# Storing the item product with the tiles innermost, so that the weights of a matmul lie 312 bytes apart

## The chip, the cores and the metric

The kernel runs on one core of one Trainium2 chip. The metric is the device time in microseconds (us), here always of that single core. TensorE does the matmuls and loads their weights (in the profile PE and PEld), VectorE is DVE, ScalarE is ACT, GpSimd is POOL, and SyncE (SP) issues most of the transfers from HBM.

## The reference

One layer of a graph network over 10000 users and 10000 items, with 128 features, all in float32:

```python
h = jnp.maximum(_layernorm(x, axis=-1), 0.0)          # [10000 users, 128]
# in the layer: user_feat = h, adj is [10000, 10000]
h = item_feat @ W_item.T + b_item                     # the item product
b = user_feat @ W_user.T + b_user
return jax.nn.relu(adj @ h + b)
# and outside: x = x + that
```

The adjacency matrix has 400 MB, and `adj @ h` is nearly all of the work.

## The kernel before

The result is made transposed: features on the 128 partitions, users along the free dimension. The users are cut into 5 groups of 2000 columns, and a group into four banks of 500 columns (`acc[0]` to `acc[3]` in PSUM). The items are cut into 78 tiles of 128, called chunks in the code, and 16 left over. For a group, TensorE goes through the 78 chunks and adds each chunk's part to all four banks.

To keep float32 precision with the `fp32r` type of TensorE, both factors are split into a high and a low part. SyncE loads an adjacency tile of 128x2000 into `a_ring` (six slots). ScalarE casts it into `hi_ring` (L277), VectorE writes the difference into `lo_ring` (L340); both rings have three slots. TensorE then does twelve matmuls of 500 columns a chunk, four for each of three products: `h_lo` by `hi_ring`, `h_hi` by `hi_ring` (both L508), `h_hi` by `lo_ring` (L514). The weights, which TensorE loads before each matmul, are `h_lo[:, c, :]` or `h_hi[:, c, :]`: for chunk `c`, 128 items on the partitions and 128 features along the free dimension. When the last of the twelve is done, the slot comes free for ScalarE.

`h_hi` and `h_lo` are the two parts of the item product. They are made once, during the first group, three chunks (a trio) at a time: three float32 matmuls L464 into a PSUM bank (each shows as two matmul rows with two weight loads), L345 on VectorE adds the bias into `h_full`, L282 on ScalarE casts it into `h_hi`, and L352 on VectorE writes `h_full - h_hi` into `h_lo`. TensorE makes the product of a trio two trios before it uses it. The other four groups only read `h_hi` and `h_lo`.

Beside that runs the layer norm of `x`, in four units a group, one in each 12 chunks. Its TensorE part is four transposes of `x` (L484), four of the normed rows (L490) and a float32 matmul with `W_user` (L497). Where the trio's matmuls L464 and the one with `W_user` fall on one chunk, L464 comes first. A group ends with the matmuls of the 16 items left over (L525), and VectorE adds the relu of the banks to `x` in `y` (L397); the first four matmuls of the next group wait for that, bank by bank.

The order on each engine is that in which the code is written; no planner chooses it. The changed lines are the two allocations of `h_hi` and `h_lo` (L104, L105). What writes them is L282 and L352, what reads them L352, L508 and L514.

Of the kernel before, what the change touches and what calls it, by code (L numbers as in the profile page):

```python
# [29 lines left out]
P = 128  # L30
N_USER = 10000
N_ITEM = 10000
HID = 128
# [10 lines left out]
CHUNKS = N_ITEM // P  # L44
# [28 lines left out]
F32R = mybir.dt.float32r  # L73
# [19 lines left out]
def graph_layer(nc, adj_tiles, adj_rem, ones_row, item_t, x_rows, w_item_t, b_item_rows, w_user_t, b_user, out_t):  # L93
    with ExitStack() as ctx:  # L94
        def sb(name, shape, dt=F32):
            return ctx.enter_context(nc.sbuf_tensor(name, shape, dt))
# [4 lines left out]
        a_ring = sb("a_ring", [P, A_SLOTS, PITCH])  # L101
        hi_ring = sb("hi_ring", [P, S_SLOTS, GROUP_W], F32R)
        lo_ring = sb("lo_ring", [P, S_SLOTS, GROUP_W], F32R)
        h_hi = sb("h_hi", [P, CHUNKS, HID], F32R)  # L104
        h_lo = sb("h_lo", [P, CHUNKS, HID], F32R)  # L105

        a_rem = sb("a_rem", [P, BANK_W])
        h_rem = sb("h_rem", [P, HID])
# [459 lines left out]
```

## Time and profile before

| | |
|---|---|
| three runs | 1153.7, 1154.68, 1154.87 us; median 1154.68 |
| the profiled execution | 1155.03 us, of which the span from first to last instruction is 1153.5 |
| mean granted TensorE clock | 0.997 |
| PE busy | 1132.1 us, 98% of the span, 5078 matmuls |
| PEld busy | 925.8 us, 80%, 5078 weight loads |
| DVE busy | 976.4 us, 85% |
| ACT busy | 773.4 us, 67% |
| read from HBM | 410.45 MB, 360 GB/s over the span |

The profile comes from one execution. A matmul's row is longer than what a matmul takes in a stream of them, because the rows of matmuls that follow each other overlap; so the step from one matmul to the next (the pitch) is read from how long a stretch of several lasts. Weight loads have rows of their own and lie beside the matmul before them. Where the trace's timeline merges rows that follow each other, "x4" is their count, and the time is from the start of the first to the end of the last.

### The profile page before, as it was taken

How to read it: one execution, taken by the hardware profiler on the slowest of the kernel's cores; microseconds unless marked ns; L12 is line 12 of the kernel's file. 1: busy time of each engine (PE TensorE's matmuls, PEld its weight loads, DVE VectorE, ACT ScalarE, POOL GpSimd, SP SyncE). 2: the span in 40 equal slices, each digit the busy share in tenths (PEclk: the TensorE clock that was granted, in tenths of full speed). 3: DMA queues.
4: the chain of work that ended last, by engine and by line, in shares of the span. 5: the costliest groups of instructions: out<-in, count | busy, mean ns of one | idle time of the engine just before them, and what ended most of it. 6: DMA issues, size and time to landing. Idle time of an engine off the chain costs nothing.

```text
span 1153.5 us, 14338 instructions
## 1 busy us (share of the span) xinstructions
PE 1132.1 (98%) x5078; PEld 925.8 (80%) x5078; DVE 976.4 (85%) x683; ACT 773.4 (67%) x502; POOL 20.3 (2%) x42
## 2 busy tenths in 40 slices
PE   6999999999999999999999999999999999999998
PEld 5888888878888888788888887888888878888886
DVE  5989988888888888898898888888888888888886
ACT  4766767667676666576667675766666657667663
POOL 0000000000000000000000000000000000000000
PEclk9999999999999999999999999999999999999999
DMA  9999999999999999999999998999999999999993
GB/s 355 397 400 359 352 364 372 347 362 345 376 372 360 367 365 392 365 370 368 355 367 362 385 379 338 376 362 373 357 371 380 381 331 378 376 358 353 364 387 120
DMA packets 62659, 416.38 MB, mean 361 GB/s; under 512 B 7644, under 2 KB 9124, under 8 KB 62608
## 3 DMA queue, kind: packets, MB, share of 16 engines
q1 hardware_dynamic: 59984, 406.38, 92.3%
q0 software_dynamic: 2624, 9.22, 2.3%
q8 instruction: 44, 0.72, 0.2%
q14 instruction: 7, 0.06, 0.0%
HBM read 410.45 MB, written 5.12 MB: 360 GB/s over the span
## 4 chain that ended last, share of the span: by engine, by line
PE 96%; DVE 1%; issue 1%; ACT 1%; DMA 1%; DVEq 0%; SPq 0%; ACTq 0%
PE acc L508 61%; PE acc L514 31%; PE spare L464 2%; PE acc L497 1%; DVE y L397 1%; PE spare L490 1%; PE spare L484 1%; ACT hi_ring L277 1%; DMA items<-in_item_t 1%; DVE lo_ring L340 0%; PE acc L525 0%; DVEq L94 0%; DVEq L427 0%; SPq L199 0%; SPq L188 0%
## 5 line engine op out<-in xcount | busy, mean ns | idle before, releaser
L340 DVE TENSOR_TENSOR lo_ring<-a_ring,hi_ring 128x2000 fp32r<-128x2000 f32 x390 | 871.3, 2241 | 152.8 <-ACT hi_ring L277 151.4
L277 ACT CAST hi_ring<-a_ring 128x2000 fp32r<-128x2000 f32 x390 | 729.0, 1869 | 360.6 <-PE acc L514 357.2
L508 PE MATMUL acc<-hi_ring,h_lo 128*128 128x500 f32 x1560 | 434.6, 399 | 5.5 <-DVE y L397 4.4
L508 PE MATMUL acc<-hi_ring,h_hi 128*128 128x500 f32 x1560 | 420.0, 391 | 0.0
L514 PE MATMUL acc<-lo_ring,h_hi 128*128 128x500 f32 x1560 | 419.1, 390 | 0.0
L508 PEld LDWEIGHTS acc<-hi_ring,h_lo 128*128 128x128 f32 x1560 | 289.5, 189 | 76.4 <-DVE y L397 12.4
L514 PEld LDWEIGHTS acc<-lo_ring,h_hi 128*128 128x128 f32 x1560 | 294.2, 189 | 62.1
L508 PEld LDWEIGHTS acc<-hi_ring,h_hi 128*128 128x128 f32 x1560 | 293.9, 188 | 61.7
L464 PE MATMUL spare<-wi,items 128*128 128x128 f32 x156 | 23.9, 294 | 10.5 <-DMA items<-in_item_t 8.7
L464 PEld LDWEIGHTS spare<-wi,items 128*128 128x128 f32 x156 | 23.0, 206 | 12.9 <-issue 6.8
L345 DVE TENSOR_TENSOR h_full<-spare,bi 128x384 f32<-128x384 f32 x26 | 14.3, 551 | 10.3 <-DMA bi<-in_b_item_rows 6.6
L245 POOL DMA_DIRECT2D rows<-in_x_rows x20 | 10.9, 544 | 595.3 <-PE spare L484 595.0
L497 PE MATMUL acc<-normed_t,wu 128*128 128x500 f32 x40 | 20.0, 581 | 0.0
L282 ACT CAST h_hi<-h_full 128x384 fp32r<-128x384 f32 x26 | 13.2, 507 | 5.5 <-DVE h_full L345 5.5
L397 DVE SCALAR_TENSOR_TENSOR y<-acc,y 128x500 f32<-128x500 f32 x20 | 12.1, 670 | 5.1 <-PE acc L525 5.1
L258 POOL DMA_DIRECT2D out_t<-y x16 | 8.8, 548 | 400.5 <-DVE y L397 399.8
L352 DVE TENSOR_TENSOR h_lo<-h_full,h_hi 128x384 fp32r<-128x384 f32 x26 | 14.4, 552 | 0.6 <-ACT h_hi L282 0.6
L364 DVE TENSOR_TENSOR centred<-rows,stat 125x512 f32<-125x512 f32 x20 | 13.9, 693 | 0.7
L387 DVE SCALAR_TENSOR_TENSOR normed<-centred,stat 125x512 f32<-125x512 f32 x20 | 13.8, 692 | 0.7
L370 DVE TENSOR_REDUCE stat<-squares 125x4 f32<-125x512 f32 x20 | 13.6, 679 | 0.0
L360 DVE TENSOR_REDUCE stat<-rows 125x4 f32<-125x512 f32 x20 | 13.6, 678 | 0.0
L287 ACT ACTIVATE squares<-centred 125x512 f32<-125x512 f32 x20 | 12.5, 627 | 0.0
(29 smaller groups left out, 113.8 us busy)
## 6 DMA issues: line engine op xcount, KB each, us to landing
a_ring<-in_adj_tiles SPq DMA_DIRECT2D x390, 1000.0 KB, 6.9
rows<-in_x_rows POOLq DMA_DIRECT2D x20, 250.0 KB, 7.6
items<-in_item_t SPq DMA_DIRECT2D x12, 384.0 KB, 7.6
out_t<-y POOLq DMA_DIRECT2D x16, 250.0 KB, 5.3
out_t<-y SPq DMA_DIRECT2D x4, 250.0 KB, 2.2
a_rem<-in_adj_rem SPq DMA_DIRECT2D x20, 31.2 KB, 4.2
items<-in_item_t SPq DMA_DIRECT2D x2, 192.0 KB, 4.9
wi<-in_w_item_t SPq DMA_DIRECT2D x1, 64.0 KB, 1.8
```

The lines of the kernel that those rows point to most:

```text
L277: nc.scalar.copy(hi_ring[:, r, :], a_ring[:, s, 0:GROUP_W]).then_inc(hi_written, 1)
L340: nc.vector.tensor_tensor(lo_ring[:, r, :], a_ring[:, s, 0:GROUP_W], hi_ring[:, r, :], ALU.subtract).then_inc(lo_written[s], 1)
L345: nc.vector.tensor_tensor(h_full[:, trio % H_BANKS, :, :], h_banks[trio % H_BANKS][:, 0:TRIO_W].rearrange("p (c d) -> p c d", d=HID), bi[: ...
L352: nc.vector.tensor_tensor(h_lo[:, trio * TRIO:(trio + 1) * TRIO, :], h_full[:, trio % H_BANKS, :, :], h_hi[:, trio * TRIO:(trio + 1) * TRI ...
L360: nc.vector.reduce_sum(total, rows[:, :, :], AX_X).then_inc(chain, 1)
L364: nc.vector.tensor_tensor(centred[:, :, :], rows[:, :, :], mean.unsqueeze(2).broadcast_to(wide), ALU.subtract).then_inc(centred_ready, 1)
L387: nc.vector.scalar_tensor_tensor(out=normed[:, :, :], in0=centred[:, :, :], scalar=0.0, in1=rstd.unsqueeze(2).broadcast_to(wide), op0=ALU.max,
L397: nc.vector.scalar_tensor_tensor(out=cols, in0=acc[k][:, 0:BANK_W], scalar=0.0, in1=cols, op0=ALU.max, op1=ALU.add).then_inc(y_ready[k], 1)
L464: last = nc.tensor.matmul(bank[:, m * HID:(m + 1) * HID], items[:, slot, at:at + P], wi[:, :], start=(m == 0), stop=True, skip_group_check ...
L497: nc.tensor.matmul(acc[k][:, 0:BANK_W], wu[:, :], normed_t[:, :], start=False, stop=False, skip_group_check=True)
L508: nc.tensor.matmul(acc[k][:, 0:BANK_W], h_part[:, c, :], hi_ring[:, r, k * BANK_W:(k + 1) * BANK_W], start=(c == 0 and h_part is h_lo), st ...
L514: last = nc.tensor.matmul(acc[k][:, 0:BANK_W], h_hi[:, c, :], lo_ring[:, r, k * BANK_W:(k + 1) * BANK_W], start=False, stop=False, skip_gr ...
```

## The change

The two tiles have their dimensions in another order: before, `[128 partitions, 78 chunks, 128 features]`, so that the 128 features of a chunk lie side by side, 4 bytes apart. Now they are `[128 partitions, 128 features, 78 chunks]`, so that the 78 chunks of one feature lie side by side, and the features of one chunk 78 x 4 = 312 bytes apart. The names `h_hi` and `h_lo` are now rearranged views with the old order of indices, so that every line that uses them stays as it is. The size in memory is the same, 39,936 bytes a partition for each of the two.

```diff
-        h_hi = sb("h_hi", [P, CHUNKS, HID], F32R)
-        h_lo = sb("h_lo", [P, CHUNKS, HID], F32R)
+        h_hi_cols = sb("h_hi_cols", [P, HID, CHUNKS], F32R)
+        h_lo_cols = sb("h_lo_cols", [P, HID, CHUNKS], F32R)
+        h_hi, h_lo = h_hi_cols[:, :, :].rearrange("p d c -> p c d"), h_lo_cols[:, :, :].rearrange("p d c -> p c d")
```

No instruction is added, removed or moved on any engine. In the profile of the changed kernel the tiles are called `h_hi_cols` and `h_lo_cols`, and each line after L105 has a number one higher.

## Rows read from the trace of the kernel before

**Rows 1.** The page: busy time, and the chain that ended last.
```profile
PE 1132.1 (98%) x5078; PEld 925.8 (80%) x5078; DVE 976.4 (85%) x683; ACT 773.4 (67%) x502; POOL 20.3 (2%) x42
PE 96%; DVE 1%; issue 1%; ACT 1%; DMA 1%; DVEq 0%; SPq 0%; ACTq 0%
```

**Rows 2.** The page's groups: line, engine, operation, shapes, count | busy us, mean ns | idle before.
```profile
L340 DVE TENSOR_TENSOR lo_ring<-a_ring,hi_ring 128x2000 fp32r<-128x2000 f32 x390 | 871.3, 2241 | 152.8 <-ACT hi_ring L277 151.4
L277 ACT CAST hi_ring<-a_ring 128x2000 fp32r<-128x2000 f32 x390 | 729.0, 1869 | 360.6 <-PE acc L514 357.2
...
L508 PEld LDWEIGHTS acc<-hi_ring,h_lo 128*128 128x128 f32 x1560 | 289.5, 189 | 76.4 <-DVE y L397 12.4
L514 PEld LDWEIGHTS acc<-lo_ring,h_hi 128*128 128x128 f32 x1560 | 294.2, 189 | 62.1
L508 PEld LDWEIGHTS acc<-hi_ring,h_hi 128*128 128x128 f32 x1560 | 293.9, 188 | 61.7
```

**Rows 3.** Timeline of PE in the third group: start us, us, line, count.
```profile
602.39 1.06 PE L508 MATMUL acc<-hi_ring,h_hi 128*128 128x500 f32 x4
603.29 1.07 PE L514 MATMUL acc<-lo_ring,h_hi 128*128 128x500 f32 x4
604.21 1.07 PE L508 MATMUL acc<-hi_ring,h_lo 128*128 128x500 f32 x4
605.12 1.06 PE L508 MATMUL acc<-hi_ring,h_hi 128*128 128x500 f32 x4
606.02 1.07 PE L514 MATMUL acc<-lo_ring,h_hi 128*128 128x500 f32 x4
```

**Rows 4.** Longest L508 matmul (min/median/max ns); timeline near the start, before the clock rose.
```profile
L508 PE MATMUL acc<-hi_ring,h_hi x1560: 384/389/620, 16.8 to 1145.7; 128*128 128x500 f32 x195
...
16.82 1.87 PE L508 MATMUL acc<-hi_ring,h_hi 128*128 128x500 f32 x4
...
16.41 1.58 PEld L508 LDWEIGHTS acc<-hi_ring,h_hi 128*128 128x128 f32 x4
```

**Rows 5.** Weight loads by line (L508, L477, L484): ns min/median/max; 128, 16, 128 columns.
```profile
L508 PEld LDWEIGHTS acc<-hi_ring,h_lo x1560: 186/188/334, 14.9 to 1144.6; 128*128 128x128 f32 x195
...
L477 PEld LDWEIGHTS spare<-wi,items_rem x2: 93/94/96, 243.8 to 243.8; 128*16 128x16 f32 x2
...
L484 PEld LDWEIGHTS spare<-ident,rows x4: 137/139/142, 600.8 to 601.3; 125*128 125x128 f32 x4
```

**Rows 6.** One trio's item product and what follows it: durations of L464, timeline of PE and PEld.
```profile
L464 PE MATMUL spare<-wi,items x6: 270/275/275, 25.3 to 25.9; 128*128 128x128 f32 x6
...
25.30 0.83 PE L464 MATMUL spare<-wi,items 128*128 128x128 f32 x6
25.88 1.16 PE L508 MATMUL acc<-hi_ring,h_lo 128*128 128x500 f32 x4
26.88 1.07 PE L508 MATMUL acc<-hi_ring,h_hi 128*128 128x500 f32 x4
...
25.08 0.86 PEld L464 LDWEIGHTS spare<-wi,items 128*128 128x128 f32 x6
25.85 0.76 PEld L508 LDWEIGHTS acc<-hi_ring,h_lo 128*128 128x128 f32 x4
```

**Rows 7.** Matmuls of the transposes and of `W_user`: durations, timeline of PE.
```profile
L484 PE MATMUL spare<-ident,rows x4: 267/268/270, 601.1 to 601.4; 125*128 125x125 f32 x4
...
601.07 0.59 PE L484 MATMUL spare<-ident,rows 125*128 125x125 f32 x4
601.41 1.14 PE L508 MATMUL acc<-hi_ring,h_lo 128*128 128x500 f32 x4
...
71.08 1.00 PE L497 MATMUL acc<-normed_t,wu 128*128 128x500 f32 x2
...
L497 PE MATMUL acc<-normed_t,wu 128*128 128x500 f32 x40 | 20.0, 581 | 0.0
```

**Rows 8.** Start of the second group, the last of the four waits of L508.
```profile
256.50 0.19 PEld L508 LDWEIGHTS acc<-hi_ring,h_lo 128*128 128x128 f32 x1 [0.40 <-DVE y L397]
```

**Rows 9.** Groups that touch the tiles once, and the slowest row an element.
```profile
L352 DVE TENSOR_TENSOR h_lo<-h_full,h_hi 128x384 fp32r<-128x384 f32 x26 | 14.4, 552 | 0.6 <-ACT h_hi L282 0.6
...
L282 ACT CAST h_hi<-h_full 128x384 fp32r<-128x384 f32 x26 | 13.2, 507 | 5.5 <-DVE h_full L345 5.5
...
L241 POOL TENSOR_SCALAR_AFFINE_SELECT ident<-ident 125x125 f32<-125x125 f32 x1 | 0.3, 287 | 0.2 <-POOL ident L239 0.2
```

**Rows 10.** Windows, one layer-norm unit of the first group: stretch, PE, PEld, DVE, ACT, POOL busy us.
```profile
50.00:86.70 36.70, 36.70 (x178) 30.58 (x177) 33.52 (x32) 25.45 (x20) 0.53 (x1) 1.00 1.01 403
```

## The prediction

> **What bounds the kernel now.** I read the chain of waits first. It lies on TensorE for 96% of the span, and TensorE is busy for 98% of it [rows 1]. The groups say the same from the other side: ScalarE sat idle for 357 us until TensorE gave a slot back, and VectorE for 151 us until ScalarE had cast [rows 2]. So both have slack, and the adjacency tiles, which wait for VectorE, come in time. The time is the number of matmuls by their pitch.
>
> The pitch comes from the timeline. From 603.29 to 606.02, one whole chunk, are 12 matmuls in 2.73 us, so 0.2275 us each [rows 3]. 4680 matmuls (3 x 1560) by that are 1065 us of the 1153.5; the rest is the first 15 us, the item product, the layer norm and the turns of the groups.
>
> Each matmul has a weight load of 189 ns [rows 2], which lies under the matmul before it. This load is what the change touches, 4680 times, and the question is how much longer it may become before it shows. Its row splits in two. 128 columns take 188 ns and 16 columns 94 ns [rows 5], so a column takes (188 - 94) / 112 = 0.84 ns, 128 of them 107 ns, and 81 ns are fixed. The fixed part does not add to the pitch: in the item product, L464, six matmuls and their six loads of 128 columns go at (0.83 - 0.275) / 5 = 0.111 us each [rows 6], though each load's row is as long as any other. So loads can follow each other at the time of their columns plus at most 4 ns. In the main stream a load may thus grow from 107 to about 223 ns of columns (2.1 times) before the pitch of 227 moves.
>
> **The price of a column 312 bytes from the next.** No row of the trace has such a read by TensorE, so I bound it. The low end is no change, 0.84 ns. For it speaks that the loads of the transposes, also 128 columns of float32, take 139 ns [rows 5], by the same fixed part 0.45 ns a column: what brings the weights can go twice as fast as L508 and L514 ask, and has something to lose before a load is longer. For the high end I take the slowest rate an element of any row, GpSimd's select, 287 / 125 = 2.3 ns with its start counted in [rows 9]. The middle of the two is 1.57 ns. I take a doubling, 1.68 ns, which is the nearest whole step: a load's columns then take 213 ns and its row 189 + 107, about 295 ns.
>
> Two pages of the Trainium skill bear on this, and they pull apart. "SBUF — State Buffer" (the note on cachelines) has lines of 16 bytes and wants at least two hits in each for full speed; at 312 bytes every column is in a line of its own. "Vector Engine (DVE) Microarchitecture Reference" (The SBUF access granule) gives VectorE prices for hops at every element, 1.73 to 1.76 ns at most distances and 2.50 at one of 96 bytes; if TensorE paid the first, a load would have 224 ns of columns and the pitch would just move, and at 2.50 it would be 325 ns. "TensorE: Matmul & The Clock Gate" (LDWEIGHTS) on the other hand gives the load as its columns over 1.2 GHz, with nothing about distance; by it the sum is zero. The trace agrees with that page on 107 ns, but only for words that lie side by side.
>
> **The change part by part, at the doubled column.**
>
> Main stream: 213 + 4 = 217 ns of load against a pitch of 227. It stays hidden, with 10 ns to spare: 0. At the low end 0 too. At the high end 128 x 2.3 + 4 = 298 ns is 71 ns over the pitch, and 4680 x 71 ns = 332 us.
>
> After short matmuls: here the cover is thin. The first load of L508 after the item product starts at 25.85, with the last matmul of L464, which lasts 107 to 111 ns; the next load already starts 0.11 us later, since four loads take 0.76 us here and 0.87 elsewhere [rows 6]. A load of 213 ns has about 106 ns uncovered, and TensorE pays them, since it is the bound. The same holds behind the transposes: (0.59 - 0.27) / 3 = 0.107 us each, and the first L508 stands directly behind [rows 7]. The places: 24 trios in the first group's loop, less the four (chunks 18, 30, 42 and 54) where the matmul of `W_user` comes between, are 20; 1 for the 16 items left over (L477); 20 behind L484 and 20 behind L490. 61 places by 0.107 us are 6.5 us. The four where L497 comes between cost nothing, since that matmul has a pitch of (1.00 - 0.58) = 0.42 us [rows 7]. At the low end this is 0, at the high end 61 x (298 - 111) ns = 11 us.
>
> Group turns: the load of the first L508 of each bank waits for VectorE and starts only then [rows 8]. The first three lie beside VectorE's next bank (0.40 us of idle time between); the last delays the chain by 0.107 us. 4 turns: 0.4 us.
>
> Before the clock rose: at the granted half clock (1.2 of 2.4 GHz) four matmuls take 1.87 us, a pitch of (1.87 - 0.62) / 3 = 0.417, with loads whose row is 333 ns [rows 4]. A load has 0.417 us of cover there. 0.
>
> The writers: L282 on ScalarE and L352 on VectorE now write, and L352 also reads, with 312 bytes between elements, 384 elements, 26 times each. VectorE's rate is 2241 / 2000 = 1.12 ns and ScalarE's 0.93 [rows 2]. At the low end nothing; at 2.3 ns, 0.45 us more for L352 and 0.53 for L282. In a layer-norm unit of the first group, 36.7 us with four trios, VectorE is busy for 33.5 and ScalarE for 25.5 [rows 10]. VectorE has 3.2 us to spare against 4 x 0.45 = 1.8, ScalarE 11.2 against 2.1. Their results are also wanted two trios later, 17 us. Hidden: 0. Were VectorE's cover gone in the four units, it would be up to 4 x 1.8 = 7 us. The first trio's casts are done before the first adjacency tile has come.
>
> The sum: 0 + 6.5 + 0.4 = 6.9 us on the profiled execution's 1155.03, gives 1161.9. The median of the runs is 0.35 us below the profiled one, so 1161.6.
>
> **The rivals.**
>
> *The columns cost what they cost now.* The reserve of two in the path of the weights [rows 5] covers the distance. Loads stay at 189 ns, and the time is 1154.7, give or take 1. For it speaks the 0.45 ns of the transposes; against it that these read neighbouring words too. 0.31.
>
> *The load becomes the bound of the main stream.* From 1.74 ns a column on (223 / 128), the pitch is the load's. This is a second mechanism beside my small term, and it has a steep price: each tenth of a nanosecond a column is 12.8 ns a matmul, 60 us. At three times the present column, 320 + 4 = 324 ns, it is 97 ns by 4680, 454 us, and with the places behind short matmuls (61 x 213 ns = 13 us) 1622. For it speaks that the doubled value lies only 3% under the point where it begins. Just above it, at 1.78 ns, it would be 23 us more, 1185. 0.12 for just above (1165 to 1200), 0.10 for far above.
>
> *The load disturbs the matmul's own reading.* 500 columns at 2.4 GHz are 208 ns, and the pitch is 227; at half clock it is 417, 500 columns at 1.2 GHz [rows 3, 4]. So something takes 19 ns a matmul at the full clock. If that is the load taking turns with the moving columns, a load that takes twice as long would take twice the turns: 19 x 4680 = 89 us more, 1251 with the 6.9; a third of that gives 1191. Against it: the matmuls with float32 columns show just 4 or 5 ns over their columns with as many loads, though at half the rate. 0.09.
>
> *Faster.* The same 19 ns may be a conflict between neighbouring words, which another layout may relieve; a tenth of it, 2 ns a matmul, is 9 us less, 1146. Nothing in the profile points to it. 0.04.
>
> *The change doesn't do what it says.* The rows of each engine are the same in kind and number, and a hidden copy into the old layout would have to be an instruction. Within the 0.31.
>
> **How the numbers follow.** My forecast, doubled or partly raised columns with the exposed places, has 0.34: 1158 to 1164 (at 1.3 ns a column the exposed part is half, some 3.5 us). Columns as now 0.31, just above the pitch 0.12, far above 0.10, disturbance 0.09, faster 0.04. A measurement of this kernel tells 0.2%, 2.3 us, from no change. Slower than that: 0.34 + 0.12 + 0.10 + 0.09 = 0.65; within: 0.31; faster: 0.04. The range reaches from 1152 to 1230: it holds the two likeliest, the load just above the pitch and a third of the disturbance, together 0.80. The likeliest one's own range is 1158 to 1164.
>
> **What would show it.** The loads of L509 and L515 (one line lower in the new file) at about 295 ns and those of L464 still at 192; the main stream still at 2.73 us a chunk; the four loads of the first L509 behind L464 no longer shorter than the others; L352 and L282 longer, without a wait behind them. If the load's row stays at 189, the first rival is right and all of my term goes. If a chunk takes more than 2.75 us, one of the two expensive rivals holds: the load as bound if its row is over 305 ns, disturbance if it is not.

## The result: slower by 7%, and the profile after

| | before | changed |
|---|---|---|
| timed runs, median | 1154.78 us (1153.7 to 1155.36) | 1236.02 us (1235.25 to 1237.7) |
| profiled execution, and its span | 1155.03, 1153.5 us | 1235.25, 1233.7 us |
| PE busy | 1132.1 us, 98% | 1214.5 us, 98% |
| PEld busy | 925.8 us, 80% | 1193.4 us, 97% |
| DVE, ACT busy | 976.4, 773.4 us | 984.7, 785.3 us |

The ratio is 1.0708, with a 95% interval from 1.0692 to 1.0724. The forecast was 1161.6 us, with a range up to 1230.

The groups of the page after answer to [rows 2] and [rows 9] (line, engine, operation, shapes, count | busy us, mean ns | idle before):

```profile
L509 PEld LDWEIGHTS acc<-hi_ring,h_lo_cols 128*128 128x128 f32 x1560 | 415.9, 331 | 17.1 <-DVE y L398 10.1
L509 PEld LDWEIGHTS acc<-hi_ring,h_hi_cols 128*128 128x128 f32 x1560 | 415.4, 332 | 0.5
L515 PEld LDWEIGHTS acc<-lo_ring,h_hi_cols 128*128 128x128 f32 x1560 | 415.3, 332 | 0.3
L465 PEld LDWEIGHTS spare<-wi,items 128*128 128x128 f32 x156 | 23.3, 208 | 11.7 <-issue 7.4
...
L283 ACT CAST h_hi_cols<-h_full 128x384 fp32r<-128x384 f32 x26 | 23.3, 897 | 6.1 <-DVE h_full L346 6.1
L353 DVE TENSOR_TENSOR h_lo_cols<-h_full,h_hi_cols 128x384 fp32r<-128x384 f32 x26 | 22.7, 872 | 0.9 <-ACT h_hi_cols L283 0.9
```

A weight load of the changed tiles takes 332 ns instead of 189; the loads of L465, whose weights lie side by side, are as before. Before, the loads of L514 had 62 us of gaps, now those of L515 have 0.3: a load follows a load without a gap. That fits loads that everything waits for, but does not show it: in the run at 12 bytes below the gaps are 0.3 us too, and there the loads are too short to be the bound. What shows it are the runs with fewer columns.

The timeline of one chunk in the fourth group (start us, us, line, count), to be laid beside [rows 3]:

```profile
803.16 1.14 PE L509 MATMUL acc<-hi_ring,h_lo_cols 128*128 128x500 f32 x4
804.14 1.14 PE L509 MATMUL acc<-hi_ring,h_hi_cols 128*128 128x500 f32 x4
805.11 1.13 PE L515 MATMUL acc<-lo_ring,h_hi_cols 128*128 128x500 f32 x4
806.08 1.00 PE L498 MATMUL acc<-normed_t,wu 128*128 128x500 f32 x2
```

From 803.16 to 806.08 a chunk takes 2.92 us where it took 2.73, so the pitch is 243.3 ns instead of 227.5. 4680 x 15.8 ns are 74 us, give or take 4, since 0.01 us in a chunk is 4 us in all. Over the whole trace at full clock, the mean pitch of the matmuls in mid-stream went from 227.5 to 244.1 ns, which is 78 us. The places behind short matmuls (for [rows 6]):

```profile
25.23 1.33 PE L509 MATMUL acc<-hi_ring,h_lo_cols 128*128 128x500 f32 x4
26.40 1.14 PE L509 MATMUL acc<-hi_ring,h_hi_cols 128*128 128x500 f32 x4
```

Before, the four long matmuls behind L464 took 25.88 to 26.88, 1.00 us, where four others took 0.91; now they take 1.17, where four others take 0.97. That is 0.11 us lost beyond the main stream's share. Over the 60 such places of the trace at full clock, the step from the first long matmul to the second went from 312 to 441 ns; less the 16 of any matmul this is 113 ns, 6.9 us for 61 places. With 0.4 us for the turns of the groups the terms are 78 + 6.9 + 0.4 = 85.

Against them stands the clock. TensorE's granted clock (third number from the end; 0.50 is 1.2 of 2.4 GHz) is half in two stretches inside the work before, and in one after:

```profile
702.20:705.50 3.30, 3.27 (x8) 2.67 (x9) 2.13 (x1) 0.00 (x0) 1.20 (x3) 0.50 0.99 385
927.50:930.80 3.30, 3.30 (x9) 2.63 (x9) 1.14 (x1) 0.75 (x1) 0.33 (x1) 0.50 1.00 385
...
273.20:276.50 3.30, 3.30 (x8) 2.57 (x9) 2.42 (x2) 0.00 (x0) 1.50 (x3) 0.50 0.95 361
```

The slow start also lasted until 19.4 us before and 17.2 after. That is 5.7 us less at half the pace, worth 2.6 us (an estimate from the pitches of 417 and 227.5 ns). Some 82 us are thus expected and the spans differ by 80.2; the last 2 were not found. VectorE's wait for ScalarE grew from 151 to 224 us, ScalarE's for TensorE from 357 to 425, both by having more slack.

### The profile page after: what moved, and what is told of

It is laid out like the page before. It is cut to its first block, busy times and chain, and to the rows that moved or that the text cites. A ratio compares the mean times of both kernels' runs of the same rounds, so it can differ in the third digit from the quotient of the medians.

```text
span 1233.7 us, 14338 instructions
## 1 busy us (share of the span) xinstructions
PE 1214.5 (98%) x5078; PEld 1193.4 (97%) x5078; DVE 984.7 (80%) x683; ACT 785.3 (64%) x502; POOL 20.4 (2%) x42
## 4 chain that ended last, share of the span: by engine, by line
PE 97%; issue 1%; ACT 1%; DMA 1%; DVE 1%; SPq 0%; DVEq 0%; ACTq 0%
PE acc L509 62%; PE acc L515 31%; PE spare L465 2%; PE acc L498 1%; PE spare L485 1%; PE spare L491 1%; ACT hi_ring L278 1%; DMA items<-in_item_t 1%; DVE y L398 0%; DVE lo_ring L341 0%; PE acc L526 0%; DVEq L94 0%; SPq L200 0%; SPq L189 0%; SPq L199 0%
## 5 line engine op out<-in xcount | busy, mean ns | idle before, releaser
L509 PE MATMUL acc<-hi_ring,h_lo_cols 128*128 128x500 f32 x1560 | 469.3, 423 | 3.6 <-DVE y L398 3.6
L509 PE MATMUL acc<-hi_ring,h_hi_cols 128*128 128x500 f32 x1560 | 444.6, 408 | 0.0
L515 PE MATMUL acc<-lo_ring,h_hi_cols 128*128 128x500 f32 x1560 | 444.2, 407 | 0.0
L509 PEld LDWEIGHTS acc<-hi_ring,h_lo_cols 128*128 128x128 f32 x1560 | 415.9, 331 | 17.1 <-DVE y L398 10.1
L509 PEld LDWEIGHTS acc<-hi_ring,h_hi_cols 128*128 128x128 f32 x1560 | 415.4, 332 | 0.5
L515 PEld LDWEIGHTS acc<-lo_ring,h_hi_cols 128*128 128x128 f32 x1560 | 415.3, 332 | 0.3
L465 PEld LDWEIGHTS spare<-wi,items 128*128 128x128 f32 x156 | 23.3, 208 | 11.7 <-issue 7.4
L465 PE MATMUL spare<-wi,items 128*128 128x128 f32 x156 | 24.0, 294 | 10.3 <-DMA items<-in_item_t 8.5
L283 ACT CAST h_hi_cols<-h_full 128x384 fp32r<-128x384 f32 x26 | 23.3, 897 | 6.1 <-DVE h_full L346 6.1
L353 DVE TENSOR_TENSOR h_lo_cols<-h_full,h_hi_cols 128x384 fp32r<-128x384 f32 x26 | 22.7, 872 | 0.9 <-ACT h_hi_cols L283 0.9
```

The lines of the kernel that those rows point to most:

```text
L283: nc.scalar.copy(h_hi[:, trio * TRIO:(trio + 1) * TRIO, :], h_full[:, trio % H_BANKS, :, :]).then_inc(h_hi_set, 1)
L353: nc.vector.tensor_tensor(h_lo[:, trio * TRIO:(trio + 1) * TRIO, :], h_full[:, trio % H_BANKS, :, :], h_hi[:, trio * TRIO:(trio + 1) * TRI ...
L465: last = nc.tensor.matmul(bank[:, m * HID:(m + 1) * HID], items[:, slot, at:at + P], wi[:, :], start=(m == 0), stop=True, skip_group_check ...
L509: nc.tensor.matmul(acc[k][:, 0:BANK_W], h_part[:, c, :], hi_ring[:, r, k * BANK_W:(k + 1) * BANK_W], start=(c == 0 and h_part is h_lo), st ...
L515: last = nc.tensor.matmul(acc[k][:, 0:BANK_W], h_hi[:, c, :], lo_ring[:, r, k * BANK_W:(k + 1) * BANK_W], start=False, stop=False, skip_gr ...
```

## The experiments

Two theories to begin with. A: the load is the bound; it needs about 1.9 ns a column, and the matmul waits for it. B: the load is hidden, but its separate reads disturb the reading of the 500 moving columns.

### One part alone

```diff
+        h_hi_cols = sb("h_hi_cols", [P, HID, CHUNKS], F32R)
+        h_hi = h_hi_cols[:, :, :].rearrange("p d c -> p c d")
```

and h_lo as before; the second run has it the other way round. Both compute the whole result.

> Only h_hi is stored with the tiles innermost, h_lo as before. Theory A (the strided load takes about 1.9 ns a column whatever else goes on, 244 ns for 128, and a matmul cannot start before its load is done): 3120 of 4680 matmuls go from 227 to 243.5 ns, +51 us; nothing at the places behind short matmuls, since there the first load is one of h_lo. 1206 us. Theory B (the strided load is hidden, but disturbs the reading of the 500 moving columns): also +51 us for the main stream; the two are not told apart here, it is the size of the parts that is. If the term behind short matmuls (6.9 us) doesn't exist, e1 and e2 together give the whole 81 us with 2 to 1 between them (1209 and 1182).

> Only h_lo is stored with the tiles innermost. Theory A: 1560 x 16.2 ns = 25 us, and the 61 places behind short matmuls and 4 group turns by 0.107 us, 6.9 us: 1155 + 32 = 1187 us. Without the term behind short matmuls 1180 to 1182.

Measured: 1203.27 us, ratio 1.0414 (1.0396 to 1.0431), and 1185.29 us, 1.0259 (1.0242 to 1.0276). That is 47.8 and 29.8 us, 77.6 together. Per matmul it is 15.3 ns for the 3120 of h_hi, and (29.8 - 6.9) / 1560 = 14.7 for h_lo, but 19.1 if the term behind short matmuls is left in: the shares are 1.6 to 1 and not 2 to 1. The timelines of PE behind L465 show the term itself, with h_hi alone and then with h_lo alone:

```profile
26.69 1.16 PE L509 MATMUL acc<-hi_ring,h_lo 128*128 128x500 f32 x4
27.69 1.14 PE L509 MATMUL acc<-hi_ring,h_hi_cols 128*128 128x500 f32 x4
```
```profile
25.19 1.33 PE L509 MATMUL acc<-hi_ring,h_lo_cols 128*128 128x500 f32 x4
26.35 1.06 PE L509 MATMUL acc<-hi_ring,h_hi 128*128 128x500 f32 x4
```

1.00 us as before the change, and 1.16 as after it: the term belongs to h_lo's loads, as expected. The halves add up to 3.6 us less than the whole. Both traces have one cheap step in each chunk, where the loads go over from the near part to the far one: it is 231 to 232 ns in the median and not 244, 390 times, 4.7 us in each run. In the changed kernel, which has far loads only, no such step is left.

### Theory A or B

The third product (L515) in the changed kernel with 128 of the 500 moving columns, the rest of that product left out:

```diff
-nc.tensor.matmul(acc[k][:, 0:BANK_W], h_hi[:, c, :], lo_ring[:, r, k * BANK_W:(k + 1) * BANK_W],
+nc.tensor.matmul(acc[k][:, 0:128], h_hi[:, c, :], lo_ring[:, r, k * BANK_W:k * BANK_W + 128],
```

> The changed kernel, but each matmul of the third product (lo_ring) streams only the first 128 of the 500 columns of its bank; the rest of that product is left out. Theory A: these matmuls still have a pitch of about 243 ns, since the load sets it, and the time stays at 1236 us. Theory B: with 128 columns to stream there is little left to disturb; their pitch falls to some 215 or less (the doubled load plus 4 ns), and the time to 1190 or less.

The time was 1225.14 us (ratio 1.0604, 1.0583 to 1.0626), nearer to theory A's 1236 than to theory B's 1190. One chunk in its timeline, PE and PEld:

```profile
805.83 0.97 PE L515 MATMUL acc<-lo_ring,h_hi_cols 128*128 128x128 f32 x4
806.63 1.31 PE L509 MATMUL acc<-hi_ring,h_lo_cols 128*128 128x500 f32 x4
807.77 1.14 PE L509 MATMUL acc<-hi_ring,h_hi_cols 128*128 128x500 f32 x4
808.75 0.97 PE L515 MATMUL acc<-lo_ring,h_hi_cols 128*128 128x128 f32 x4
...
805.59 1.06 PEld L515 LDWEIGHTS acc<-lo_ring,h_hi_cols 128*128 128x128 f32 x4
806.55 1.07 PEld L509 LDWEIGHTS acc<-hi_ring,h_lo_cols 128*128 128x128 f32 x4
```

The loads of L515 are (1.06 - 0.34) / 3 = 0.24 us apart (243 ns in the median over the trace), with a quarter of the columns to stream, and a chunk still takes 2.92 us, from 805.83 to 808.75. The 11 us that were saved lie where the stream changes to the short matmuls or to the next group: the stretch from the first load of L515 before such a change to the second long matmul behind it is 116 to 172 ns shorter in the median, 84 times, 11 us in all. Theory A holds at 312 bytes: the matmul has no part in the pitch.

Fewer weight columns, in the same line, are the other side of it:

```diff
+nc.tensor.matmul(acc[k][0:64, 0:BANK_W], h_hi[:, c, 0:64], lo_ring[:, r, k * BANK_W:(k + 1) * BANK_W],
```

and the same with 112 of the 128.

> The changed kernel, but each matmul of the third product loads only 64 of the 128 weight columns (and makes 64 of the 128 features; the rest of that product is left out). Theory A: a load of 64 strided columns takes 122 ns, its row about 205, well under a matmul of 227, so the 1560 matmuls that have such a load beside them go back to 227 ns: 1236 - 25 = 1211 us. Theory B: half the strided reads, half the disturbance: a pitch of 235 and 1223 us.

> The changed kernel (312 bytes), but each matmul of the third product loads only 112 of its 128 weight columns (and makes 112 features; the rest of that product is left out). With the load as bound, at 1.87 ns a column, 112 columns are done in 209 + 4 = 213 ns, below the matmul's 227. If the pitch of 243.7 is the load's alone, it falls at once to the 229 to 232 that the hidden strided loads show (64 columns, and 320 bytes): 1236 - 1560 x 13 ns = 1216 us. If the pitch follows the number of strided reads in proportion instead: 227 + 16.5 x 112 / 128 = 241.5, and 1233 us.

Both leave out the features whose weights are not loaded. Measured: 1214.13 us (ratio 1.0509, 1.0488 to 1.053) and 1218.37 (1.055, 1.0511 to 1.0589). The timeline of PE with 112 columns, and its loads on the page of groups with 64 and with 112:

```profile
806.50 1.09 PE L515 MATMUL acc<-lo_ring,h_hi_cols 128*112 128x500 f32 x4
807.42 1.14 PE L509 MATMUL acc<-hi_ring,h_lo_cols 128*128 128x500 f32 x4
```
```profile
L515 PEld LDWEIGHTS acc<-lo_ring,h_hi_cols 128*64 128x64 f32 x1560 | 313.5, 201 | 37.0 <-issue 1.1
```
```profile
L515 PEld LDWEIGHTS acc<-lo_ring,h_hi_cols 128*112 128x112 f32 x1560 | 388.2, 291 | 1.2
```

From 128 to 112 strided columns the pitch falls at once, from 243 to 0.92 / 4 = 230 ns here and 232 in the mean of the trace, and 112 down to 64 bring only 4 us more in 1560 matmuls, 3 ns each (229 in the mean; the times alone, two executions each, do not tell the two apart). That is a threshold, as theory A has it: 1216 was expected for it, and 1233 for a price in proportion.

The rows confirm the price. 81 + 64 x 1.87 = 201 ns and 81 + 112 x 1.87 = 290 are the rows of 201 and 291; 128 columns would have 320, and the row is 332. Where the loads are the bound, a row is thus some 12 ns longer than its fixed part and its columns.

### How far apart is far

All these compute the whole result; only the order in memory differs, so that the weights lie at other distances. Of each edit, the line that sets the order (the lines that use the tiles are adapted to it):

```diff
+ h_both = sb("h_both", [P, CHUNKS, HID, 2], F32R)          # 8 bytes, h_hi = [..., 0], h_lo = [..., 1]
+ h_hi = sb("h_hi", [P, TRIOS, HID, TRIO], F32R)            # 12 bytes, h_lo alike
+ h_both = sb("h_both", [P, TRIOS, HID, TRIO * 2], F32R)    # 24 bytes
+ h_hi = sb("h_hi", [P, HID, CHUNKS + 2], F32R)             # 320 bytes, h_lo alike
```

> h_hi and h_lo are stored interleaved, so that the 128 weights of a matmul lie 8 bytes apart: each line of 16 bytes still holds two of them. Theory L (lines: a load is slow when fewer than two of its columns share 16 bytes): loads stay at 189 ns, pitch 227, 1155 us. Theory N (neighbours: any column that is not adjacent to the one before costs about 1.9 ns): loads of 332 ns, pitch 243.5 and 1236 us.

> Three chunks are stored innermost, the weights of a matmul lie 12 bytes apart: 128 columns touch 96 lines of 16 bytes. Theory L: between the two; at 1.9 ns a line 96 lines are 182 ns, so the load's row grows to about 260 ns, which the matmul still hides; only the 61 places behind short matmuls show, 75 ns each: 1155 + 5 = 1160 us. Theory N: 1236 us.

> Three chunks and the two parts are stored innermost, the weights of a matmul lie 24 bytes apart, each in a line of its own. Theory L and theory N: as in the changed kernel, loads of 332 ns and 1236 us. If the distance itself matters (a price that grows with it), something between 1160 and 1230.

> As the changed kernel, but the row of chunks is padded from 78 to 80, so that the weights lie 320 bytes apart, a multiple of 16 and of 64, and all columns of a load lie at the same place in their line. If the price of 1.9 ns holds for any far column: 1236 us. If 312 bytes suffered from its odd alignment, less; if 320 meets a conflict between banks of the memory, far more (2.5 ns a column would be a pitch of 324 ns and 1620 us).

The first three went as the lines of 16 bytes would have it in their order, but not in size: 1160.33, 1167.41 and 1185.17 us, where theory L had 1155, 1160 and 1236. 320 bytes were the surprise: 1181.67 us, not 1236. So more distances, with h_hi alone in rows of 82, 84 and 79 chunks, and both parts with 39 or 156 columns to a row:

> Only h_hi is stored with the tiles innermost, in rows padded to 82 chunks, so that its weights lie 328 bytes apart, 8 more than a multiple of 16, as 312 are. With the same in rows of 78 the time was 1203, a pitch of 243.5 ns for 3120 matmuls. If it is the place in the line (columns alternately at two places of their line) that makes 312 bytes dearer than 320: again 243 ns and about 1203 us. If it is something particular to 312: loads of about 301 ns and a pitch of 231.5, 1155 + 3120 x 4.4 ns = 1169 us.

> As the last, with rows of 84 chunks, 336 bytes, an odd multiple (21) of 16 where 320 is an even one (20). If only the place in the line counts: as 320, loads of about 301 ns and 1169 us. If lines an odd number apart are dearer: 1190 to 1203 us.

> Both parts with 39 chunks innermost, 156 bytes between the weights, half of 312. If far columns fall into two classes, 1.7 ns (24, 320, 328 bytes) and 1.9 ns (312, 336 bytes): either about 1184 us with loads of 301 to 308 ns, or about 1236 with 325 to 332. A price that grows with the distance from 24 on is already excluded by 320 and 328; 156 tells only which class is the rule.

> Both parts in one tile, the high part's 78 chunks and then the low part's 78 in each row, so that the weights lie 624 bytes apart, twice 312. As for 156 bytes: 1184 us or 1236 us by class. If distances beyond some size are dearer still, more than 1250.

> Only h_hi with the tiles innermost, rows padded to 79 chunks, 316 bytes: the columns come at all four places of a line in turn. Between 312 (pitch 243.5, 1203 us) and 320 (231.6, about 1169 us). If the classes go by single distances, one of the two; if they go by regions, since 312 and 320 differ, something between, about 1186.

| bytes between weights | parts | load row, ns (third product) | time, us | ratio, 95% interval |
|---|---|---|---|---|
| 4 (before) | both | 189 | 1154.78 | |
| 8 | both | 196 | 1160.33 | 1.0047 (1.003 to 1.0064) |
| 12 | both | 253 | 1167.41 | 1.011 (1.0093 to 1.0127) |
| 24 | both | 308 | 1185.17 | 1.0272 (1.0255 to 1.0289) |
| 156 | both | 349 | 1278.13 | 1.1067 (1.1031 to 1.1103) |
| 312 (the change) | both | 332 | 1236.02 | 1.0708 (1.0692 to 1.0724) |
| 320 | both | 301 | 1181.67 | 1.0239 (1.0222 to 1.0256) |
| 624 | both | 308 | 1176.30 | 1.0186 (1.0155 to 1.0216) |
| 312 | h_hi | 332 | 1203.27 | 1.0414 (1.0396 to 1.0431) |
| 316 | h_hi | 305 | 1176.38 | one run, see below |
| 328 | h_hi | 308 | 1168.84 | 1.012 (1.0091 to 1.0149) |
| 336 | h_hi | 329 | 1198.17 | 1.0374 (1.0344 to 1.0404) |

Of the 316 bytes there are two timed executions, 1176.38 us (the profiled one) and 6399.81. The second is told here and not used; nothing shows what held it up. The two expected classes, 1184 and 1236 us, did not hold either: 156 bytes are dearer than both and 624 cheaper.

The loads' rows, with the fixed 81 ns taken off, leave 115 ns of columns at 8 bytes, 172 at 12, and 220 to 227 at 24, 320, 328 and 624. Counted in lines of 16 bytes, the 128 columns lie in 64, 96 and 128 of them, which is 1.8, 1.8 and 1.7 to 1.8 ns a line; side by side (32 lines) the 107 ns of the columns themselves are longer. So a price for each line fits every short distance and several long ones (305 ns at 316 bytes is another), though at 1.8 ns and not at the 1.9 that theory L took from 312 bytes. The Trainium skill says as much in "SBUF — State Buffer" (the note on cachelines): full speed needs two hits in a line of 16 bytes, and each step to a new line has its price. With two hits, the trace has 196 ns against 189, nearly free. The Trainium skill's "Vector Engine (DVE) Microarchitecture Reference" (The SBUF access granule) has hops free only behind adjacent pairs of words. TensorE's loads of every second word, 8 bytes apart, cost 7 ns in all, so that stricter rule is VectorE's and not this path's.

156, 312 and 336 bytes cost more: 268, 251 and 248 ns by their rows, or, since rows are too long where the loads are the bound, 248, 239 and 238 by the steps between loads (252, 243 and 242 ns) less 4. It isn't the place within a line: in the changed kernel the columns of chunk c begin 4c bytes further on, and over c modulo 4 the mean load of h_hi is 332.0, 332.0, 333.0 and 332.6 ns in its trace. Nor is it 8 bytes beyond a multiple of 16 (328 is cheap), nor an odd number of lines (624 is 39 of them, and cheap). Which distances are dear stays open.

### A hidden load is not free

At 320 bytes the load's row is 301 ns, and yet 27 us were lost. In the timeline of PE:

```profile
803.85 1.08 PE L516 MATMUL acc<-hi_ring,h_lo 128*128 128x500 f32 x4
804.77 1.09 PE L516 MATMUL acc<-hi_ring,h_hi 128*128 128x500 f32 x4
805.70 1.08 PE L522 MATMUL acc<-lo_ring,h_hi 128*128 128x500 f32 x4
806.62 1.00 PE L505 MATMUL acc<-normed_t,wu 128*128 128x500 f32 x2
```

2.77 us a chunk, a pitch of 230.8 here and 231.6 in the mean of the trace. Is that the load's own? The same edit to 128 moving columns tells:

> The kernel with rows of 80 chunks (320 bytes), and each matmul of the third product streams only 128 of its 500 columns, the rest of that product is left out. It shows the load's own pitch at 320 bytes. If the pitch of 231.5 ns with full matmuls is the load's (load as bound): again 231 ns. If loads of 301 ns are really hidden and the other 4.5 ns are a disturbance of the moving columns: loads 220 to 226 ns apart in the third product.

It took 1151.41 us (ratio 0.9977, 0.9957 to 0.9998), with the rest of the third product left out. Its timeline, PE and PEld:

```profile
805.70 1.11 PE L516 MATMUL acc<-hi_ring,h_hi 128*128 128x500 f32 x4
806.64 0.88 PE L522 MATMUL acc<-lo_ring,h_hi 128*128 128x128 f32 x4
...
806.41 0.96 PEld L522 LDWEIGHTS acc<-lo_ring,h_hi 128*128 128x128 f32 x4
```

In the clear the loads follow each other at (0.96 - 0.31) / 3 = 0.217 us, and at 219 ns in the median over the trace. That is 1.66 to 1.68 ns a column with the 4 ns between loads taken off, and about 9 ns below the pitch of 227.5 that the matmul had before; still the full matmuls come at 231. So beside theory A, theory B has a small share: strided reads that stay under the matmul cost it some 4 ns. (That the moving columns slow the load down instead, to 231, is not excluded at 320 bytes; at 312 they do not, with 243 to 244 ns between loads either way.) At 12 bytes, with a load of 253 ns, a chunk is 806.15 to 808.90 in its timeline, 2.75 us, some 2 ns a matmul; that load has 50 ns to spare, so there it can only be the disturbance. At 24, 316, 328 and 624 bytes the matmuls beside far loads come at 230 to 234 ns, and no run shows the load's own pitch.

Does the load beside it also make up the 19 ns that the matmul had over 208 before?

```diff
+nc.tensor.matmul(acc[k][0:32, 0:BANK_W], h_hi[:, c, 0:32], lo_ring[:, r, k * BANK_W:(k + 1) * BANK_W],
```

in the kernel before, with the other 96 features of the third product left out.

> The kernel before the change, but each matmul of the third product loads only 32 weight columns (and makes 32 of the 128 features; the rest of that product is left out). If the 19 ns by which the pitch exceeds 500 columns at 2.4 GHz come from the load beside it: a pitch near 213 ns where loads of 32 columns are beside the matmul, and 1155 - 1560 x 14 ns = 1133 us. If they belong to the moving columns themselves: 227 ns and 1155 us.

1146.95 us, ratio 0.9929 (0.9899 to 0.9959). Two chunks of its timeline:

```profile
805.39 1.05 PE L514 MATMUL acc<-lo_ring,h_hi 128*32 128x500 f32 x4
806.28 1.07 PE L508 MATMUL acc<-hi_ring,h_lo 128*128 128x500 f32 x4
...
808.09 1.07 PE L514 MATMUL acc<-lo_ring,h_hi 128*32 128x500 f32 x4
809.00 1.06 PE L508 MATMUL acc<-hi_ring,h_lo 128*128 128x500 f32 x4
```

Four matmuls of L514 take 0.89 us in one and 0.91, as any other four, in the next. Over the whole trace, the matmuls that have a load of 32 columns beside them have a mean pitch of some 225 ns against 227 for the same ones before. So about 2 of the 19 ns go with the load, far from the 14 expected, and the others stay. What they are was not found. The 8 us that the run gained are only in part those: in its profiled execution the granted clock never fell inside the work, where it did so twice in the one before.

## Why the prediction was wrong

The step that failed is the price of a column. I bounded it by 0.84 and 2.3 ns, took the doubling, 1.68, for no better reason than that it is a whole step, and so put the main stream at 0, with 10 ns to spare. The changed kernel's columns take (243.3 - 4) / 128 = 1.87 ns, and the main stream pays some 16 ns a matmul. That is 11% over my value and 7% over the 1.74 from which, as I wrote, the load becomes the bound. The runs put that point between 1.68 ns (320 bytes) and 1.87, and the price behind it is steep: 11% in one term turned 7 us into 81. The rival "load as the bound", just above the threshold, was the case that came, at 1236 where I had it end at 1200; its formula gives, for 1.87 ns, 4680 x 15.8 ns and some 8 us for the places, 1237 us in all. I gave it 0.12 and the range ended at 1230. With the chosen value 3% under a point where each tenth of a nanosecond is 60 us, and with no row for the price, half of the chance should have stood above that point and the range should have reached past it.

Step by step:
- What bounds the kernel: right. TensorE kept 98%, all else had more slack.
- The split of the load's row into 81 ns and 0.84 ns a column, and that loads follow each other at their columns plus 4 ns: right. In the run with loads of 32 columns the row is 108 ns, which is 81 + 32 x 0.84; at 312 bytes, 112 columns stayed under the matmul and 128 did not.
- The chosen doubling: wrong for 312 bytes. That it fits 320 bytes, 1.66 to 1.68 ns in the clear, is luck; no rule that I had tells the two apart.
- Hidden means free: wrong too, by 4 ns a matmul, 20 us. At 320 bytes, where the load's own pitch is 217 ns as I had it for the change, the time is still 1181.67 and not 1161.6. This fits the rival "the load disturbs the matmul's own reading", with about a quarter of the size that I gave it (4 of 19 ns); at 12 bytes, where nothing else is left, it is 2 ns.
- The places behind short matmuls: right in kind and place, 6.5 us expected and 6.9 measured. With 1.87 ns my formula has 239 - 107 = 132 ns for a place, and 129 came, 16 of which every matmul pays.
- Before the clock rose (I read that from the pitch of 0.417 us): right, four matmuls and loads as before, a pitch of 0.417 and rows of 334 to 341 ns. That the clock falls again later, and not at the same places in two executions, was left out of the sum; it is worth 2.6 us here.
- The writers: 26 times 390 ns more for the cast on ScalarE and 320 for L353, below the bounds of 530 and 450, without a wait behind them.
- Columns as now, faster, and a change that does nothing: none of them came.

## What to carry to other kernels

A weight load that lies under a matmul has a reserve that can be read off: the pitch of the stream less the columns' part of the load. Work out from which price it is gone, and treat a value close to it as a coin toss, not as hidden. A row without gaps on PEld does not tell that it is gone; fewer columns in the moving or in the loaded operand do. Keep at least two weights in each 16 bytes: 8 bytes apart cost 0.5%, 12 bytes 1.1%, and farther ones 2 to 11% here, by a rule of distances that was not found, so that a layout with strided weights should be timed with a few paddings (two spare chunks in a row took back 54 of the 81 us).

## What the runs showed of the hardware

- At half clock the distance hardly shows. In stretches with a granted clock of 0.50 the rows of loads 4, 12, 320 and 312 bytes apart are (min/median/max ns):

```profile
L508 PEld LDWEIGHTS acc<-hi_ring,h_hi x4: 329/331/338, 702.4 to 703.6; 128*128 128x128 f32 x4
L516 PEld LDWEIGHTS acc<-hi_ring,h_hi x4: 323/330/334, 259.6 to 260.8; 128*128 128x128 f32 x4
L516 PEld LDWEIGHTS acc<-hi_ring,h_hi x4: 322/330/334, 491.3 to 492.5; 128*128 128x128 f32 x4
L509 PEld LDWEIGHTS acc<-hi_ring,h_hi_cols x4: 334/336/341, 273.7 to 275.0; 128*128 128x128 f32 x4
```

  At full clock their medians are 188, 252, 301 and 332. So the row of a near load gets much shorter with the clock and that of a load at 312 bytes hardly at all.

- At 8, 12, 24, 316, 320, 328 and 624 bytes a load costs by lines of 16 bytes, about 1.75 ns each by its row. At 156, 312 and 336 bytes it is 1.86 to 1.94, by the steps between loads.
- The profile's row of a load is 81 ns plus its columns as long as it is hidden (32 near columns 108 ns, 64 and 112 far ones 201 and 291), and some 12 ns more where the loads are the bound.
- A strided load that is short enough to be hidden still adds 2 ns (12 bytes) to 4 ns (320 bytes) to the matmul of 500 columns above it.
- 312 bytes between elements cost ScalarE's cast of 384 elements 390 ns, 1.0 ns each, and VectorE's subtraction, which both reads and writes so, 320 ns, 0.8 ns each.
